# Six sequences in flight instead of four, with shared buffers, a row-grouped mask product and a new instruction order

## The reference

```python
x = layer_norm(x + attention(x, x, causal & key mask))         # A0, LN0
x = layer_norm(x + attention(x, ctx, key mask))                # A1, LN1
x = layer_norm(x + relu(x @ w1 + b1) @ w2 + b2)                # F0, LN2
x = layer_norm(x + attention(x, ctx, mask == 0 -> -1e10))      # A2, LN3
x = layer_norm(x + attention(x, ctx, scores * side, dropped))  # A3, LN4
x = x + attention(layer_norm(x), ctx)                          # LN5, A4
x = x + attention(layer_norm(x), itself, key mask)             # LN6, A5
x = x + gelu(layer_norm(x) @ w1 + b1) @ w2 + b2                # LN7, F1

def attention(q_in, kv_in, mask):      # per head of 16 features
    scores = Q @ K.T / 4, masked;  p = softmax(scores);  return (p @ V) @ Wo + bo
```

## Time and profile before

| | us |
|---|---|
| median of 3 runs | 1294.31 (1289.99 to 1297.86) |
| profiled execution | 1289.55 |
| its span, first to last instruction | 1287.8 |
| PE busy | 1226.7 (95%) |
| PEld busy | 958.8 (74%) |
| DVE busy | 801.9 (62%) |
| ACT busy | 487.6 (38%) |
| POOL busy | 206.8 (16%) |

### The profile page before, as it was taken

One profiled execution on the slowest core, in us unless ns is written; L12 is line 12 of the kernel. 1 busy time (PEld: TensorE's weight loads), 2 busy tenths in 40 slices (PEclk: granted clock), 3 DMA queues, 4 the chain that ended last, 5 costly groups with the idle time before them and its releaser, 6 DMA issues.

```text
span 1287.8 us, 34825 instructions
## 1 busy us (share of the span) xinstructions
PE 1226.7 (95%) x14292; PEld 958.8 (74%) x14292; DVE 801.9 (62%) x2117; ACT 487.6 (38%) x1126; POOL 206.8 (16%) x319
## 2 busy tenths in 40 slices
PE   6999999999999999999999999999999999999976
PEld 4787777877778786777878777787777768777754
DVE  4546876656675666757656675675567566665731
ACT  1242323334334442543434343343434334333332
POOL 0112211112121110202112120211212121121110
PEclk9899989999999999999999999999999999999998
DMA  7400110100101010010100101010010101001000
GB/s 292 203 2 2 42 42 2 46 13 12 47 2 29 30 57 2 13 47 2 58 2 17 42 13 46 2 57 2 16 43 6 53 2 57 2 2 47 6 5 5
DMA packets 22939, 43.97 MB, mean 34 GB/s; under 512 B 6529, under 2 KB 16897, under 8 KB 19713
## 3 DMA queue, kind: packets, MB, share of 16 engines
q1 hardware_dynamic: 21824, 40.30, 8.8%
q10 hardware_dynamic: 960, 1.44, 0.3%
HBM read 39.63 MB, written 2.10 MB: 32 GB/s over the span
## 4 chain that ended last, share of the span: by engine, by line
PE 49%; issue 36%; POOL 7%; DVE 6%; DMA 1%; SPq 1%; ACT 0%; POOLq 0%; DVEq 0%
PE bank L627 13%; PE bank L620 13%; PE bank L708 5%; PE bank L660 4%; PE bank L613 4%; PE bank L685 3%; POOL root L572 3%; PE bank L653 3%; DVE neg_max L943 2%; PE bank L680 2%; POOL x_res L581 2%; POOL x_res L586 2%; POOL x_res L589 1%; PE bank L674 1%; PE bank L721 1%
## 5 line engine op out<-in xcount | busy, mean ns | idle before, releaser
L572 POOL TENSOR_TENSOR root<-var_eps,halves 128x1 f32<-128x1 f32 x128 | 72.1, 564 | 961.1 <-DVE var_eps L996 961.1
L943 DVE TENSOR_REDUCE neg_max<-bank 128x4 f32<-128x512 f32 x320 | 203.0, 681 | 36.2 <-PE bank L660 35.7
L820 ACT ACTIVATE exps_t<-bank 128x512 f32<-128x512 f32 x320 | 168.6, 607 | 108.1 <-PE bank L696 107.8
L627 PE MATMUL bank<-x_t,weights_A 128*128 128x128 f32 x1024 | 138.0, 284 | 5.0 <-ACT x_t L804 4.9
L627 PEld LDWEIGHTS bank<-x_t,weights_A 128*128 128x128 f32 x1024 | 126.6, 196 | 14.4 <-ACT x_t L804 7.4
L627 PE MATMUL bank<-x_t,weights_F 128*128 128x128 f32 x1024 | 128.3, 281 | 1.4 <-ACT x_t L804 1.4
L627 PEld LDWEIGHTS bank<-x_t,weights_F 128*128 128x128 f32 x1024 | 121.9, 195 | 7.7 <-issue 3.6
L708 PE MATMUL bank<-exps_t,v_one 128*32 128x128 f32 x3072 | 122.5, 281 | 2.1 <-ACT exps_t L820 1.7
L620 PE MATMUL bank<-weights_F,exps_t 128*128 128x256 f32 x512 | 122.4, 383 | 0.1
L660 PE MATMUL bank<-k_eo,q_t 32*128 32x256 f32 x1536 | 110.6, 401 | 1.0 <-DVE q_t L931 0.6
L620 PE MATMUL bank<-weights_A,o_t 128*128 128x256 f32 x384 | 104.4, 396 | 5.1 <-ACT o_t L827 4.8
(11 more groups left out here) (101 smaller groups left out, 1781.7 us busy)
## 6 DMA issues: line engine op xcount, KB each, us to landing
weight<-in_fside SPq DMA_DIRECT2D x16, 1024.0 KB, 4.8
weights_A<-in_weights_A SPq DMA_DIRECT2D x4, 1028.0 KB, 17.4
weights_F<-in_weights_F SPq DMA_DIRECT2D x2, 2054.0 KB, 15.1
drop_raw<-in_drop SPq DMA_DIRECT2D x16, 256.0 KB, 5.2
x_hat<-in_x SPq DMA_DIRECT2D x16, 128.0 KB, 2.0
out<-x_sum SPq DMA_DIRECT2D x16, 128.0 KB, 1.7
ctx_t<-in_ctx_t SPq DMA_DIRECT2D x13, 128.0 KB, 3.5
rows_A<-in_rows_A SPq DMA_DIRECT2D x3, 512.0 KB, 19.6
```

Of the source, the lines that this page charges most:

```text
L572: nc.gpsimd.tensor_tensor(root[x][:], var_eps[x][:], halves[:, e:e + 1], ALU.pow).then_inc(done["root"], 1)
L627: mm = nc.tensor.matmul(dst[:, 128 * f:128 * f + 128], w[:, c, 128 * f:128 * f + 128], tokens_t[:, c, :], start=(c == 0), stop=(c == KC - 1))
L820: nc.scalar.activation(dst, score_bank(x, "ST", s, j)[:], ACT.Exp, scale=DH ** -0.5).then_inc(done["exp"], 1)
L943: nc.vector.tensor_reduce(neg_max[x][:, j, :], heads, AX_X, ALU.max, negate=True).then_inc(done["max"], 1)
```

## The change

- SETS is 6: six sequences in flight, sequence x in buffer set x modulo 6.
- To make room, the exponentials (and the hidden activations, which share the buffer) use three buffers for all sequences, and o_raw two. Tables say which buffer a stage takes, and ACT waits until the previous user's last PV, Y or oT has read it.
- x_res is gone: POOL writes the residual over x_hat (after TensorE has transposed x_hat, a new wait for xT) or over x_sum. o_t shares the buffer of q_t.
- v_one is stored with 17 columns a head instead of 32; the stationary operand of L708 is still 32 columns wide and runs over into the next head's values, whose result rows nobody reads.
- In A1 the mask product of S is done by row groups: for each group of heads a product over 32 rows, with `pick[.., 0, :]` as the stationary operand, instead of one over 128 rows with the identity.
- All order tables and the table of banks are new. They group beats of the same tile form.

The diff, cut to its core (of the tables one line each way):

```diff
-SETS = 4
+SETS = 6
+EXP_BUFFERS, OUT_BUFFERS = 3, 2
+VE = DH + 1
 TENSOR = """
-12311210010020011101330000101010001101200012103030212102200010000002222201101121133011100000123312010333330123110000
+12345112100100230011101340000101010100201000212202201301222222300001002033100023104033333111102113001113202042130432
...
+def shared_places(places, beats):
+    at, before, held = {}, {}, {}
+    for (x, _, s, *_), place in zip(beats, (int(digit) for digit in "".join(places.split())), strict=True):
+        at[x, s], before[x, s], held[place] = place, held.get(place), (x, s)
+    return at, before
...
-        x_res = per_set("x_res", [128, D])
-        v_one = per_set("v_one", [128, H, 2 * DH])
+        v_one = per_set("v_one", [128, H * VE + 2 * DH - VE])
-        exps_t = per_set("exps_t", [128, H, N])
-        o_raw = per_set("o_raw", [128, GROUPS, N])
+        exps_t = [sb(f"exps_t{b}", [128, H, N]) for b in range(EXP_BUFFERS)]
+        o_raw = [sb(f"o_raw{b}", [128, GROUPS, N]) for b in range(OUT_BUFFERS)]
-        o_t = per_set("o_t", [128, KC, N])
+        o_t = q_t
...
-                load_ctx(sp, 3)
+                for x in range(3, SETS):
+                    load_ctx(sp, x)
...
                     if n in POST_NORM:
-                        nc.gpsimd.tensor_tensor(x_res[x][:], x_hat[x][:], row(s, LN[n]["g"]), ALU.mult
+                        pool.wait_ge(done["xT"], nth(x, "xT", s))
+                        nc.gpsimd.tensor_tensor(x_hat[x][:], x_hat[x][:], row(s, LN[n]["g"]), ALU.mult
                                                 ).then_inc(res_scaled, 1)
...
                         for j in range(GROUPS):
-                            nc.tensor.matmul(free_bank((x, "S", s), j)[:], idb[:], four(mask_bias(x, s)), start=True, stop=True)
+                            if s == "A1":
+                                nc.tensor.matmul(free_bank((x, "S", s), j)[:], pick[group_rows(j), 0, :],
+                                                 bias[x][group_rows(j), 1, :].unsqueeze(1).broadcast_to([32, GH, 128]),
+                                                 start=True, stop=True)
+                            else:
+                                nc.tensor.matmul(free_bank((x, "S", s), j)[:], idb[:], four(mask_bias(x, s)), start=True,
+                                                 stop=True)
...
+            def free_exponentials(engine, x, s):
+                if before := EXP_BEFORE[x, s]:
+                    y, t = before
+                    if t in FFN:
+                        engine.wait_ge(done["Y"], nth(y, "Y", t, 1))
+                    else:
+                        engine.wait_ge(done["PV"], nth(y, "PV", t, GROUPS - 1))
...
+                        if j == 0:
+                            free_exponentials(act, x, s)
...
+                        if before := OUT_BEFORE[x, s]:
+                            act.wait_ge(done["oT"], nth(before[0], "oT", before[1]))
                         act.wait_ge(done["PV"], nth(x, "PV", s, GROUPS - 1))
```

More of the change, by code:

```diff
@@ L228 @@
+464699997776698889aa7755aa999aa886b6ababbccbba979aa7ccccbbccddaabbb88dddcdccbb99ddeeccaafefeeedddffffeeffdbdbeeeccff
+feeddffeeff
 """
 SYNC = """
-000111222333012444035551466625777368887499958aaa69bbba7ccc8bddd9ceeeadfffbecfdef
+0010122123334455450123456666077718882999378aaa94abbb5ccc6bddd7cdeee8fff9eafbcdef
+"""
+EXP_PLACES = """
+21222211222112122211211222111112112000100001200212112222212211112201010012012210110110111011110000111010101100101111
+111102221122
+"""
+OUT_PLACES = """
+100001100101001000001110100101010001001111110101101001101110100011011100011100111000001000001111
@@ L285 @@
     _held |= {_bank: (_beat, _j) for _j, _bank in enumerate(BANK[_beat])}
+def shared_places(places, beats):
[3 more added lines that the diff above has]
+    return at, before
+EXP_AT, EXP_BEFORE = shared_places(EXP_PLACES, [b for b in SCALAR_ORDER if b[1] in ("exp", "h_t") and b[3] == 0])
+OUT_AT, OUT_BEFORE = shared_places(OUT_PLACES, [b for b in SCALAR_ORDER if b[1] == "o_raw"])
 WEIGHT_TURNS = [beat[0] for beat in SYNC_ORDER if beat[1] == "load_weight"]
@@ L337, in program, with in_sets @@
         sxs_bias = sb("sxs_bias", [128, 128], BF16)
+        def in_sets(made):
+            return [made[x % SETS] for x in range(B)]
         def per_set(name, shape, dt=F32):
-            return [sb(f"{name}{x}", shape, dt) for x in range(SETS)] * (B // SETS)
+            return in_sets([sb(f"{name}{x}", shape, dt) for x in range(SETS)])
         x_hat = per_set("x_hat", [128, D])
         x_sum = per_set("x_sum", [128, D])
-        x_res = per_set("x_res", [128, D])
         x_t = per_set("x_t", [128, KC, N])
@@ L387, in sems @@
         def sems(name):
-            return [sem(f"{name}{x}") for x in range(SETS)] * (B // SETS)
+            return in_sets([sem(f"{name}{x}") for x in range(SETS)])
         x_loaded = sems("x_loaded")
@@ L540, in _ @@
                 for x in range(SETS):
-                    sp.wait_ge(stored[x], 16 * (B // SETS))
+                    sp.wait_ge(stored[x], 16 * len(range(x, B, SETS)))
             @block.gpsimd
@@ L707, in outputs @@
                     for n in range(GH):
-                        mm = nc.tensor.matmul(bank((x, "PV", s, 0))[32 * n:32 * n + 32, 128 * j:128 * j + 128], v_one[x][:, head(j, n), :],
-                                              exps_t[x][:, GH * j + n, :], start=True, stop=True)
+                        mm = nc.tensor.matmul(bank((x, "PV", s, 0))[32 * n:32 * n + 32, 128 * j:128 * j + 128], v_one[x][:, VE * head(j, n):VE * head(j, n) + 2 * DH],
+                                              exps_t[EXP_AT[x, s]][:, GH * j + n, :], start=True, stop=True)
                     mm.then_inc(done["PV"], 1)
@@ L791, in free_values @@
                 engine.wait_ge(done["V"], nth(x, "V", s))
[L792 removed]
+                return (heads_of(v_one[x])[:, :, 0:DH], bank((x, "V", s))[:, 0:D].rearrange("p (h d) -> p h d", h=H))
             @block.scalar
@@ L980, in add_residual @@
                             dve.wait_ge(stored[x], 16 * (x // SETS))
-                        residual = x_hat[x]
                     else:
                         dve.wait_ge(done["res"], nth(x, "res", INPUT_LN[s]))
-                        residual = x_res[x]
+                    residual = x_hat[x] if s == "A0" or INPUT_LN[s] in POST_NORM else x_sum[x]
                     nc.vector.tensor_tensor(x_sum[x][:], src[:, 0:D], residual[:], ALU.add).then_inc(done["sum"], 1)
```

130 lines of the change are left out of this document (67 added, 63 removed).

## The result

The changed kernel takes 1227.08 us in the median (1225.34 to 1228.55, 4 runs), against 1293.23 for the kernel before. The ratio is 0.9485, with a 95% interval of 0.9453 to 0.9518. Forecast were 1227.0 and 1200 to 1260. The span of the profiled execution went from 1287.8 to 1224.7 us.

The account below looks back on a forecast made before the run. PE, busy 1226.7 of 1287.8 us, was taken to bound the kernel: 1287.8 - 26.1 - 10.4 - 32 + 4 - 3 = 1220.3 us of span, with the median then put at 1227 us, range 1200 to 1260.

Parts of the forecast that it names:

- Tile forms: On PE, 164 fewer changes of tile form (754 to 590) save 26.1 us in ends and starts of pieces.
- Mask: In A1, four row-grouped mask products run side by side on PE: 10.4 us less.
- Waits: PE's waits within the stream: six sequences lengthen distances, up to 47 us less, 32 taken; bounds 0 and 50.
- Clock: Lower clock at the end, where one sequence runs alone: 3 us of 9 lost come back; bounds 0 and 9.
- Start: First k_eo comes later behind more input and mask issues: 4 us more; bounds 0 and 8.
- (a): Rival: the waits in PE's stream stay; span 1255 us, time 1262; chance 0.17.
- (b): Rival: waits and clock go to their bounds, -50 and -9 us; span 1196, time 1203; chance 0.13.
- (c): Rival: A1's row-grouped mask products are not concurrent, 10.4 us back; 1237 us; chance 0.05.
- (d): Rival: POOL as a chain, residuals waiting for xT delay roots by 1.5 us each, 96 us; 1323 us; chance 0.03.

Follow-up runs that it names:

- a_res4: Changed kernel with an own residual buffer, and no wait of POOL for xT, for four of six buffer sets: 1226.59 us, ratio 0.9486.
- a_full_mask: Changed kernel with A1's mask product over all 128 rows again, order kept: 1236.54 us, ratio 0.9571.
- a_start: Changed kernel with all inputs issued before all masks, and mask biases of sequences 3 to 5 made right before their own k_eo: 1231.34 us, ratio 0.9513.
- a_start2: Changed kernel with the start of a_start, and A1's weights issued behind the third mask instead of the sixth: 1224.06 us, ratio 0.9460.

## Why the prediction was right

**The number.** That 1227.0 met 1227.08 is luck. The sum gave a span of 1220.3 us, and it was 1224.7. The 4.8 us by which the median of the kernel before lay above its profiled execution were added to it, but in the changed kernel that distance is 0.5. The two errors cancel. What was right is the way and the size: 67.5 us forecast, 63.1 in the profiled spans and 66 in the medians. Without the clock it was 64.5 forecast and 56 measured at full speed.

**What bounds.** PE sets the end, as read: the terms that were worked out as PE's time came.

**Tile forms.** Forecast 26.1, by the balance 26.2; but this is the same reading applied to the new order. The traces show it without that reading. For each piece without visible idle time and at the full clock, I take the time from its start to the next start, less its steps. The medians are the same in both kernels: 0.14 us for L708 (160 pieces) and L752 (94), 0.21 for L660 and L704, 0.23 for L685 and L729, 0.20 for L620 and L627 and for L655 and L662. Each median times its number of pieces, added up, gives 130.0 us before and 104.1 after: 25.9 less. The experiment with the added product has the price by itself, 0.23 us for two changes.

**Mask.** Forecast 10.4; 10.4 of steps by the balance, 10.2 between the medians in the new order. The four products take 0.21 us together where four full ones take 0.86. So the 3.07 times of the Trainium skill ("TensorE: Matmul & The Clock Gate", section "Measured speedup vs the span model"), which the prediction quotes, is less than this trace shows: here it is four times.

**Waits.** This is the mis-sized term: forecast 32, measured 20.8. Counting the work between a beat and its successor said that 47 us would go, and the discount of a third was too small. One part of the error is in the count: its 84 us of missing distance were set against 77 us of rest, but only 49.3 us of that is idle time of PE, and the other 27 did not move. Another may be DVE's queue, which no count of TensorE's order sees: added DVE work reached TensorE, but work taken away brought little. The discount was explained by the in-place residual and by o_raw; the first cost nothing where it was undone (a_res4). The wait for o_raw is 6.3 us in 4 places (9.4 in 5 by the order), and the exponentials' buffers cost no wait, as forecast; neither was undone in a run. No run has six sequences in the old grouping or the new grouping with four, so that the waits fell by distance is argued from the order, not shown.

**Clock.** Forecast 3, measured 7.2 in the profiled spans and 10 over the executions. It makes up for much of what the waits lacked, and the total was right by that. At the end, where the 3 us were forecast, the term went from 8.9 to 5.1, so that reading was good. The rest came in the first 300 us, which the prediction did not count: there 17 us at the lower level became 10 (8.5 and 5.1 us lost).

**Start.** Forecast 4 later, k_eo came 3.2 later (21.28 against 18.07). PE's idle time in it grew by 1.5 only, since the transposes of five sequences stand ahead of K where those of three did, and that work has to be done anyway. The prediction took the whole delay as a loss.

**The rivals.** (a), waits stay, and (b), waits go to their bound, both fall by the balance: a quarter of the 77 us went. (c) falls by a_full_mask. (d) is a mechanism of the old order (10 us), not of the new one.

## What to carry to other kernels

Where TensorE is nearly full, price a piece of work from start to start, once between its own tile form and once between others, and count pieces in the order: that gave more than half of this gain, and the new trace has the same prices within about 0.01 us. Waits counted as missing distance on one engine are an upper bound; here less than half of it came (20.8 of 47 us). Compare clock losses over several executions, not between two profiles. A wait that is taken away at the start must be followed to the next transfer, and the granted clock behind it read as well.

## What was not expected

- The same edit was worth 10.2 us in one order and 5.9 in the other, and a part of that difference is the clock.
- A start that was quicker for K made a slower kernel: the granted clock was 0.86 on average in the first 30 us of a_start against 1.00 in the changed kernel. That it was the 5.48 us wait which brought it down was seen in this trace and, shorter (3.4 us behind a wait of 2.41), in that of a_start2, not isolated.
- The clock also falls where TensorE is never idle. In the changed kernel it does so at 295.4 us, within a run of 32 rows that are products of one column (the first line), and stays down for 6.8 us:

```profile
293.01 4.65 PE L765 MATMUL bank<-weights_F 128*128 128x1 f32 x32
```
```profile
295.40:302.20 6.80, 6.80 (x35) 5.17 (x35) 2.15 (x4) 0.00 (x0) 0.93 (x1) 0.50 0.01 2
```

  In the kernel before it falls at 188.0 us, within the same run of L721, and for as long. No run takes these products away.
- DVE load is asymmetric: 65 us more cost 22, 33 us less brought 3.
